# Clearing the block-diagonal buffer in eight GpSimd instructions of 256 columns instead of one of 2048

## The reference

```python
def reference(x, ctx_512, ...):
    x = x + _L0_xattn_ref(_layernorm(x), ctx_512, ...)              # 16 heads of 8: causal self + cross attention
    x = x + _L0_ffn_ref(_layernorm(x), ...)                         # 8 experts, top 2 of a router
    x = x + _L1_xattn_ref(_layernorm(x), ctx_512, ctx_512, ...)     # one head of 128 over the context
    x = x + _L1_ffn_ref(_layernorm(x), ...)                         # the block below
    return x

def _L1_ffn_ref(x, Wq, Wk, Wv, Ws, Wd, Wo):                         # H, DH, E, K = 16, 64, 8, 2
    gate_v = jnp.einsum('btc,hec->bthe', x, Ws)
    w, sel = jax.lax.top_k(gate_v, K)
    mix_v = jnp.einsum('bthk,bthke->bthe', jax.nn.sigmoid(w), jax.nn.one_hot(sel, E))
    v = jnp.einsum('bthe,bted->bhtd', mix_v, jnp.einsum('btc,edc->bted', x, Wv))
    probs = jax.nn.softmax(jnp.einsum('bhid,bhjd->bhij', q * scale, k), axis=-1)
    attn = jnp.einsum('bhij,bhjd->bihd', probs, v)
    mask_o = jax.nn.one_hot(jax.lax.top_k(jnp.einsum('btc,hec->bthe', x, Wd), K)[1], E).sum(axis=3)
    return jnp.einsum('bthe,bthd,efd->bthf', mask_o, attn, Wo).sum(axis=2)
```

## Time and profile before

| | |
|---|---|
| median of 3 runs | 1322.04 us (1322.01 to 1323.66) |
| the profiled execution | 1322.67 us |
| its span, first to last instruction | 1320.9 us |
| TensorE busy | 1137.6 us, 86% |
| VectorE / ScalarE / GpSimd busy | 706.6 / 494.1 / 85.0 us |
| mean granted TensorE clock | 0.847 of full speed |

### The profile page before, as it was taken

One profiled execution on the slowest core, in us unless ns is written; L12 is line 12 of the kernel. 1 busy time (PEld: TensorE's weight loads), 2 busy tenths in 40 slices (PEclk: granted clock), 3 DMA queues, 4 the chain that ended last, 5 costly groups with the idle time before them and its releaser, 6 DMA issues.

```text
span 1320.9 us, 21222 instructions
## 1 busy us (share of the span) xinstructions
PE 1137.6 (86%) x8499; PEld 883.2 (67%) x8499; DVE 706.6 (53%) x1867; ACT 494.1 (37%) x1022; POOL 85.0 (6%) x134
## 2 busy tenths in 40 slices
PE   6888779989989988989988988988998998985696
PEld 4547545777668765877577855976577766874475
DVE  5514466646565557547665658546664656423500
ACT  4233415352534425451634334442535253422120
POOL 0010002000110002000200011000200011000000
PEclk8558959899789979998889978998889978977556
DMA  7000000242020420142022221042023210133222
GB/s 212 0 1 4 3 0 1 48 69 65 8 49 17 69 55 21 29 76 57 6 49 47 47 47 46 5 77 63 1 48 67 64 40 13 29 56 84 52 44 52
DMA packets 198032, 56.85 MB, mean 43 GB/s; under 512 B 173568, under 2 KB 193838, under 8 KB 197934
## 3 DMA queue, kind: packets, MB, share of 16 engines
q1 hardware_dynamic: 195630, 51.20, 19.9%
q10 hardware_dynamic: 2304, 4.29, 1.1%
HBM read 31.36 MB, written 24.12 MB: 42 GB/s over the span
## 4 chain that ended last, share of the span: by engine, by line
PE 75%; DVE 11%; ACT 7%; issue 3%; SPq 3%; DMA 2%; ACTq 0%; DVEq 0%
PE bank L928 10%; PE bank L737 10%; PE bank L773 9%; PE bank L884 5%; PE bank L663 5%; PE bank L843 4%; PE bank L624 3%; PE bank L678 3%; PE bank L588 3%; DVE negmax L1261 3%; ACT pa L1022 3%; PE bank L942 2%; PE bank L860 2%; PE bank L688 2%; PE bank L911 2%
## 5 line engine op out<-in xcount | busy, mean ns | idle before, releaser
L1022 ACT ACTIVATE pa<-bank 128x512 f32<-128x512 f32 x224 | 123.4, 596 | 122.8 <-PE bank L678 75.8
L1261 DVE TENSOR_REDUCE negmax<-bank 128x2 f32<-128x512 f32 (+1 forms) x224 | 139.0, 683 | 41.9 <-PE bank L526 22.1
L1039 ACT ACTIVATE pa<-bank,b_c 128x256 f32<-128x256 f32 x256 | 107.5, 471 | 128.6 <-PE bank L737 127.3
L928 PE MATMUL bank<-vb,pb 128*128 128x65 f32 x1024 | 137.1, 299 | 4.2 <-issue 4.2
L928 PEld LDWEIGHTS bank<-vb,pb 128*128 128x128 f32 x1024 | 132.8, 214 | 10.3 <-issue 7.9
L737 PE MATMUL bank<-xnT_a,w 128*128 128x256 f32 x512 | 138.1, 417 | 0.1
L773 PE MATMUL bank<-w,pa 128*128 128x128 f32 x1024 | 124.2, 276 | 0.0
L773 PEld LDWEIGHTS bank<-w,pa 128*128 128x128 f32 x1024 | 121.9, 192 | 3.2
L1101 ACT ACTIVATE pb<-bank 128x512 f32<-128x512 f32 x128 | 69.9, 602 | 125.4 <-PE bank L888 125.4
L737 PEld LDWEIGHTS bank<-xnT_a,w 128*128 128x128 f32 x512 | 101.1, 208 | 17.3 <-ACT pa L1039 0.5
L1415 DVE TENSOR_REDUCE negc<-bank 128x2 f32<-128x512 f32 x128 | 80.0, 684 | 58.8 <-PE bank L860 58.6
(11 more groups left out here) (240 smaller groups left out, 1706.3 us busy)
## 6 DMA issues: line engine op xcount, KB each, us to landing
v_d<-at SPq DMA_DIRECT2D x32, 256.0 KB, 3.3
vb<-v_d SPq DMA_DIRECT2D x32, 256.0 KB, 6.0
at_d<-at SPq DMA_DIRECT2D x32, 256.0 KB, 2.1
at<-at_d SPq DMA_DIRECT2D x32, 256.0 KB, 4.4
pv_d<-pvs SPq DMA_DIRECT2D x8, 512.0 KB, 3.1
pvs<-pv_d SPq DMA_DIRECT2D x16, 256.0 KB, 4.2
w<-in_L_ffn_W_dram ACTq DMA_DIRECT2D x1, 2048.0 KB, 11.5
bd<-mix_d SPq DMA_DIRECT2D x128, 8.0 KB
```

The lines of the kernel that those rows point to most:

```text
L928: mm = pe.matmul(BB[2 + qt][:, i * (DH + 1):(i + 1) * (DH + 1)], pb[:, h % NPB, kt * T + qt * P:kt * T + (qt + 1) * P], vb[:, kt, h, :], s ...
L1022: nc.scalar.activation(pa[:, e % NPA, :], BA[e % 2][:, :], ACT.Exp, scale=SC0).then_inc(S["a_ex"], 1)
L1039: ins = nc.scalar.activation(hT[:, u % 4, c, :], BA[u % 2][:, c * T:(c + 1) * T], ACT.Relu, bias=b1_c[:, k:k + 1])
L1261: nc.vector.tensor_reduce(negmax[:, i:i + ng], BA[j][:, :].rearrange("p (g k) -> p g k", g=ng), AX, ALU.max, negate=True).then_inc(S["a_mx ...
```

## The change

Each of the two memsets becomes a loop of eight over 256 columns, every one of which increments `b_bz`. The counts that SP waits for, and the number per sequence, go up by the factor eight: SP still waits until the whole buffer is clear. Nothing is moved: the eight stand in GpSimd's queue where the one stood, and the other engines' queues are the same instruction for instruction.

```diff
-            b_mx=16, ..., b_pr=32, b_bz=2, b_md=32, ...
+            b_mx=16, ..., b_pr=32, b_bz=16, b_md=32, ...
...
                     def b_fill(_):
                         sp.wait_ge(S["b_md"], upto("b_md", 32))
-                        sp.wait_ge(S["b_bz"], upto("b_bz", 1))
+                        sp.wait_ge(S["b_bz"], upto("b_bz", 8))
...
                     def b_sel(_):
-                        sp.wait_ge(S["b_bz"], upto("b_bz", 2))
+                        sp.wait_ge(S["b_bz"], upto("b_bz", 16))
...
+                    def clear_blocks():
+                        for i in range(8):
+                            nc.gpsimd.memset(bd[:, 256 * i:256 * i + 256], 0.0).then_inc(S["b_bz"], 1)
+
                     def b_gates(_):
                         if now[0] == 0:
                             pool.wait_ge(s_spread, N_SPREAD)
                         if now[0] > 0:
                             pool.wait_ge(S["b_z"], upto("b_z", 0))
-                        nc.gpsimd.memset(bd[:, :], 0.0).then_inc(S["b_bz"], 1)
+                        clear_blocks()

                     def b_mix(half):
                         if half == 1:
                             pool.wait_ge(S["b_mm"], upto("b_mm", 2 * NT))
-                            nc.gpsimd.memset(bd[:, :], 0.0).then_inc(S["b_bz"], 1)
+                            clear_blocks()
```

More of the change, by code:

```diff
@@ L218, in transformer_program @@
             b_xn=1, b_xt=1, b_xc=1, b_x1=1, b_g=1, b_gc=1, b_sg=1, b_pvj=2, b_pvc=2, b_qkp=8, b_hi=8, b_lo=8, b_s=16,
-            b_mx=16, b_ct=1, b_cc=1, b_st=16, b_ex=16, b_mw=1, b_pd=16, b_pr=32, b_bz=2, b_md=32, b_dm=256, b_do=128,
+            b_mx=16, b_ct=1, b_cc=1, b_st=16, b_ex=16, b_mw=1, b_pd=16, b_pr=32, b_bz=16, b_md=32, b_dm=256, b_do=128,
             b_mm=4, b_ve=4, b_vd0=32, b_vd1=32, b_vr=64, b_pv=8, b_at=8, b_ad=64, b_ar0=32, b_ar1=32, b_z=2, b_zc=2, b_ro=2, b_xo=2,
```

## The result

The changed kernel takes 1397.3 us (median of six runs, 1379.5 to 1419.9), the kernel before on the same chip 1322.0 us (six runs, 1318.9 to 1323.7). The medians are 75.3 us apart. The ratio is 1.051, with a 95% interval of 1.044 to 1.058: 5.1% slower, or 67 us. The forecast was 1343, with a range of 1320.5 to 1350. The profiled execution is the longest of the six, 1419.9 us with a span of 1418.2, 97.3 us above the span of before.

The account below looks back on a forecast made before the run. TensorE, busy 86% of the span, was taken as the bound, with `vb`'s transfer setting `b_attend(0)` and hiding the collision. 1322.7 us plus 21 of low clock gave 1343.7, 0.6 above the median basis: 1343, range 1320.5 to 1350.

Parts of the forecast that it names:

- What bounds the kernel, and the collision: At the second memset, q = 0 to 5: DVE's pair is blocked, losing 1.45 us each, mostly hidden behind `vb`'s transfer.
- Eight memsets for one, at no cost: At both zeroings: eight memsets take 2.06 us instead of 1.80, and nobody waits for the 0.26 us more.
- DVE gets in after one piece or two: At the second zeroing: DVE's pair ends by 0.71 us after the start, so `xn_a` comes 1.24 us earlier.
- rival B: At the second zeroing: GpSimd does not give way between pieces, `xn_a` 0.26 us late; +1.6 us, 1323.6; chance 0.27.
- TensorE at `b_attend(0)` 9.8 us after the memset, `vb` unmoved, a wait of 2.4 us: Before the first L928, q = 0 to 5: TensorE arrives earlier, gains 0.2 us and stands 2.4 us for `vb`.
- The clock falls behind that wait, on work that nothing hides: Behind the `vb` wait, q = 0 to 5: granted clock drops to 0.50 where the chain has TensorE alone; chance 0.55.
- How long it stays low: Behind the `vb` wait: 8.5 us of low clock per sequence, the middle between 3.4 and 13.5.
- The term of +21 us: Six sequences, q = 0 to 5: 3.8 us lost to low clock less 0.2 gained, 3.6 us each.
- The price of 0.45 us for each us of low clock: TensorE at half speed: each microsecond loses about 0.45, read from q = 6 of the kernel before.
- q = 6 and q = 7 unchanged: The last two sequences: no effect expected; in q = 6 no collision, in q = 7 cover of 1.4 us.
- C: At the `vb` wait: DVE gets through but the clock holds; only 1.2 us gained, 1320.8; chance 0.12.
- D: At the L928 group: the time gained before `b_attend(0)` is kept in full; -16.5 us, 1305.5; chance 0.06.

Follow-up runs that it names:

- `whole_late`: Kernel before, both memsets whole, the second waiting until DVE has finished `xn_a` (q = 0 to 6): 1395.1 us, ratio 1.046.
- `split_first`: Kernel before with only the first memset of each sequence (in `b_gates`) in eight pieces: 1322.9 us, ratio 1.0003.
- the fillers: Changed kernel with unused matmuls before `b_attend(0)`, five in q = 0 to 5, nine in q = 6: 1327.7 us at 512 columns, 1315.7 at 256.
- `split_second`: Kernel before with only the second memset of each sequence (in `b_mix`) in eight pieces: 1389.4 us, ratio 1.052.
- `split_dense_later`: Changed kernel with six unused matmuls of 512 columns before `b_attend(1)` in q = 0 to 5: 1385.7 us, ratio 1.049.
- `split_reorder`: Changed kernel with `b_attend(0)` and `b_score(4)` placed behind `c_out` and `f_stack(7)`: 1320.9 us, ratio 0.998.
- `split_two`: Changed kernel with two memsets of 1024 columns instead of eight of 256, in both places: 1395.9 us, ratio 1.051.
- the reordered kernels: `b_attend(0)` and `b_score(4)` placed behind `c_out` and `f_stack(7)`: 1320.9 us on the changed kernel, 1341.0 us on the kernel before.

## Why the prediction was right and wrong

- *What bounds the kernel, and the collision*: right. Undoing it by other means (`whole_late`) does what the split does.
- *Eight memsets for one, at no cost*: right, 1.0003 in `split_first`. They take 2.08 us when alone (2.06 forecast), and 2.22 to 2.26 beside DVE.
- *DVE gets in after one piece or two*: right, and rival B (0.27) is refuted. 0.50 us in four sequences, 0.71 in two; 0.71 was forecast.
- *TensorE at `b_attend(0)` 9.8 us after the memset, `vb` unmoved, a wait of 2.4 us*: right, 9.8 to 10.0 and 2.1 to 2.9. Right also that behind the transposes the clock no longer falls (1.00 from 287.0 to 297.2), and that L928 gains 0.2 us.
- *The clock falls behind that wait, on work that nothing hides*: right in kind, and the fillers show that it is the whole loss. The Trainium skill, page "TensorE: Matmul & The Clock Gate", section "HAM oscillation — how this bites in real kernels", describes waits for DMA that send the engine back to half rate, so that the next piece of work starts slow. The trace agrees in kind: 0.50 from 298.3 on, 1.0 us after the end of a wait of 2.55 us. What the prediction says of q = 6 there is not exact: its clock fell 1.0 us before the wait of 4.00 us ended, not at its end.
- *How long it stays low*: wrong. The step that failed is "I take 8.5 us of low clock per sequence, the middle between 3.4 and 13.5". It measured 58.0 us in four sequences and 13.7 in two (6.8 us more following); over the span the low clock grew by 35 us per sequence in the profiled execution, and by 20 in that of `split_second`. The term of +21 us came out at 97.3 us in the profiled execution and at 67 by the ratio. The bounds were the only two stretches that I had read behind a wait, and I took them for the ends of what is possible. The trace of before already had a much longer one, on other work, in q = 7 (81.9 us, shown behind this list), and q = 0 and q = 1 of the changed kernel show that they are not the ends on this work either: behind waits of 2.55 and 2.35 us the same instructions follow, and the clock is back after 58.0 us in the one and 13.7 in the other. In the 58 us TensorE is busy 56.87 of 57.80 us all the same. With the six matmuls of 512 columns in their way, in `split_dense_later`, none lasted longer than 17.1 us. Why the stretches have the lengths that they have stays open.
- *The price of 0.45 us for each us of low clock*: right, 212 us more of it against 97.3 us of span, 0.46.
- *q = 6 and q = 7 unchanged*: right, 92.3 us against 92.2.
- *Rivals C and D*: both were real possibilities of this kernel that need something more than the split. What C describes comes about once the wait is filled; its gain of 1.2 us can't be told from nothing. D asked that `vb` land before TensorE comes, and it never did land earlier. That 1303.5 us is close to D's 1305.5 is partly luck: some 6 us of it are q = 6, which D left alone, and the six sequences of `split_reorder` win 13.2 us where D had 16.5.

The stretch in q = 7 of the kernel before, all of it at half speed:

```profile
1232.00:1313.80 81.80, 62.08 (x390) 54.72 (x390) 12.74 (x30) 11.87 (x21) 1.80 (x1) 0.50 0.30 55
```

**What stays open.** Why waits so alike give 58, 13.7 or 10.2 us. Over the 24 waits in q = 0 to 5 of the changed kernel, `split_second`, `whole_late` and `split_two` (1.8 to 3.2 us), the moment of the fall sorts them: 0.85 to 1.32 us after L928's start it is 58.0 us (13 waits), at 1.43 to 1.46 it is 13.7 (5 waits), at 0.76 or sooner it is 10.2 (6 waits). The six of `split_dense_later` fit: falls at 0.2 to 0.4 us gave 10.2, those at 1.1 to 1.3 us lasted until the added matmuls. q = 6 of the reordered kernels doesn't: the clock fell 2.2 us after L928's start in one and 1.1 before it in the other, and both stretches were 51.2 us. A few tenths of a microsecond seem to decide over 14 us, and the starts vary by as much with the DMAs. By the rows by sequence above, one long stretch in place of a short one is 14.6 us, so by this estimate two or three of them more or fewer would be the 40 us between the runs. But no run moved the fall alone, so this is an observation, not a cause.

## What to carry to other kernels

When you remove a stall, look up what the engine will wait for next, and what its clock does behind that wait; a stall of 2 us that is followed by work behind a transfer may be the cheapest place to stand. If the profile shows the next wait to be a transfer, put the engine's own later steps into the gap in the same change: here the split alone cost 67 us, and the split with two steps moved and one gap filled won 19, of which filling that gap was worth 6 by itself. And when a cost rests on how long a clock stays low, the longest stretch read so far is no upper bound; here the same instructions behind like waits had stretches of 10.2, 13.7 and 58.0 us.

## What was unexpected of the hardware

- Each of 24 waits of 1.8 to 3.2 us in front of L928 went with a fall of the clock, and 13 of them, of 2.0 to 2.9 us, with 58.0 us at 1.2 GHz. In q = 0 of the changed kernel TensorE was busy 56.87 of 57.80 us in it. In `split_reorder` a wait of 2.89 us was followed by 51.2 us of it.
- Five matmuls of 256 columns (2.43 us in all) in the gap kept the clock up; in q = 0 no low clock followed for 31 us, and the ratio to the kernel before went from 1.051 to 0.995.
- DVE's pair was held by a memset of 1.80 us that started 0.10 us after it, but got in behind the first memset of 0.31 us (in two of six sequences the second) though more followed without a break. With two memsets of 1024 columns it got in behind the first of those.
